# Attention probabilities turned by a DMA transpose of two f16 halves instead of by TensorE, with new periods for all engines

## The chip, the cores and the metric

The kernel runs on one core of one Trainium2 chip. The metric is the device time of one launch in microseconds (us); lower is better.

## What is computed

64 graphs of 128 nodes with 384 features pass through four layers of graph attention with residuals and layer norms. The last two layers (numbers 4 and 5 in the code, parts "c") have 12 heads of 32 features. For each of them the reference does, per graph,

```
score = q @ k.T * scale + bias        # 12 heads, 128 x 128 each
prob  = exp(score - max(score))       # softmax, divided later by its row sum
out_h = prob @ v_h / sum(prob)        # per head
```

All is f32. The kernel gets f32 accuracy from f16 matmuls by splitting each operand in a high half (its f16 rounding) and a low half (the rest, in f16) and adding three products. TensorE (PE) sums over the partitions, so `prob @ v` needs `prob` turned, with the column index on the partitions.

## The kernel before

**Tiling.** One graph is one tile of 128 partitions (nodes) x 384. Its work is cut into streams: "a" and "w" are the first layer pair, "b" and "x" the second, "c" and "y" layers 4 and 5, with small streams for the norms, the masks, the biases and the splits. The 12 heads are handled as four quads j = 0 to 3 of three heads (chunks c = 0 to 2), one PSUM bank (`c_banks[j]`) for a quad.

**Order.** Each engine issues its instructions in the order of a period that is written out as a string in `ORDER`: each letter is the next step of that stream. `FIRST` says in which period and at which place a stream starts, so in one steady period the engines work on steps of about four successive graphs. The function `woven` (L243) issues the periods. An engine runs strictly in this order, so a wait at one step holds all behind it. `WARM_FIRST` and `WARM_LAST` put filler matmuls (L590, L594) into the first and last periods; in the steady part there are none. SyncE (SP), which issues all DMAs, has no period: weights and biases first, then per graph the loads (L268, L273, L278) and the store (L282).

**The steps around the change**, per layer (4 and 5) and graph, with the names of `quad(layer, j)` signals:

- PE L527 makes the scores of the four quads, 24 matmul records for 12 heads.
- VectorE (DVE) L1010 scales them and adds the bias into `score`, L1015 takes the negative row maximum of each head.
- ScalarE (ACT) L739 makes `prob` with Exp, three instructions a quad.
- PE L386 (helper `turned`, called at L534) turns the f32 `prob` of a quad by three transposes into `c_banks[j]`.
- ACT L610 (from L799) copies the bank to f16 as `pt_hi`; DVE L828 (from L1038) writes the rest as `pt_lo`.
- PE L542 to L544 multiply with `v`, nine small matmuls a quad, into bank `c0`; DVE L1042 and L1052 divide by the row sums.

The order within a graph closes a loop: the scores of layer 4 of the next graph wait for `head_out_ready` of layer 5 of this one (L523).

Of the kernel before, what the change touches and what calls it, by code (L numbers as in the profile page):

```python
# [54 lines left out]
def gnn_stack_kernel(nc, x, adj, adj_turned, w_t, biases, norm_rows, beta, out, graphs):  # L55
# [8 lines left out]
    with ctx:  # L64
# [35 lines left out]
        scaled_a, affine_a = (sb(n, [128, D]) for n in ("scaled_a", "affine_a"))  # L100
# [24 lines left out]
        pt_hi = sb("pt_hi", [128, QUADS, CHUNKS, 128], f16)  # L125
        pt_lo = sb("pt_lo", [128, QUADS, CHUNKS, 128], f16)
# [137 lines left out]
        def _(sp):  # L264
# [53 lines left out]
            for m in range(9, N_W):  # L318
                load_weight(m)
# [897 lines left out]
```

## Time and profile before

| | |
|---|---|
| time, median of 3 runs | 2939.22 us (2938.55 to 2939.28) |
| span of the profiled execution | 2938.2 us |
| around the span | 1.0 us, the median less the span |
| PE, DVE, ACT, POOL busy | 2901.9, 2549.3, 2344.3, 393.0 us |
| granted TensorE clock, mean | 0.999 of full |

"Busy" is the share of time in which at least one instruction of the engine runs. Matmuls overlap, so the cost of one is read from the distance between starts in the timeline, not from its duration. Durations of DVE, too, overlap a little with the next one.

### The profile page before, as it was taken

Reading aid. Unit: us, or ns where it says so; the run is one execution under the profiler, and the core shown is the slowest. Engines: PE = TensorE matmul, PEld = TensorE weight load, DVE = VectorE, ACT = ScalarE, POOL = GpSimd, SP = SyncE. Lnnn points to the kernel's source line nnn. Section 1 sums busy time; section 2 is a strip of 40 time slices with the busy share of each in tenths; the row PEclk is TensorE's granted clock in tenths of the full one; section 3 lists DMA queues with packets and bytes.
Section 4 is the critical chain, followed back from the end, with each engine's and each line's share of the span. In section 5 each row is a group of like instructions: output and inputs, shape, how many; then the busy total and the mean of one; then the engine's idle time right before and its main releaser. Section 6 shows DMA issues by size and latency. Waiting matters only on the chain.

```text
span 2938.2 us, 89028 instructions
## 1 busy us (share of the span) xinstructions
PE 2901.9 (99%) x35033; PEld 2323.2 (79%) x35033; DVE 2549.3 (87%) x7450; ACT 2344.3 (80%) x6548; POOL 393.0 (13%) x715
## 2 busy tenths in 40 slices
PE   8999999999999999999999999999999999999998
PEld 6777877877878778787777778778778787787877
DVE  6788888888888898888888888888888888988886
ACT  6788878878878888878888888788788788888775
POOL 1111111111111111111111111111111111111110
PEclk9999999999999999999999999999999999999999
DMA  6000000000000000000000000000000000000000
GB/s 217 11 16 12 14 15 13 14 15 13 13 16 13 13 14 15 13 13 13 16 13 13 15 12 14 15 13 14 15 13 13 16 13 13 13 15 13 13 8 7
DMA packets 48621, 54.21 MB, mean 18 GB/s; under 512 B 5712, under 2 KB 48208, under 8 KB 48208
## 3 DMA queue, kind: packets, MB, share of 16 engines
q1 hardware_dynamic: 48208, 48.52, 5.2%
q8 instruction: 282, 4.62, 0.7%
q14 instruction: 131, 1.07, 0.1%
HBM read 35.92 MB, written 12.58 MB: 17 GB/s over the span
## 4 chain that ended last, share of the span: by engine, by line
PE 94%; DVE 3%; issue 1%; ACT 1%; DMA 1%; SPq 0%; POOL 0%; POOLq 0%; ACTq 0%; DVEq 0%
PE bank_a L340 27%; PE bank_c L340 23%; PE bank_b L340 19%; PE bank_c L386 8%; PE bank_b L372 4%; PE bank_b L379 2%; PE bank_c L527 2%; PE bank_b L386 2%; PE bank_a L386 1%; DVE node_b L968 1%; PE bank_c L543 1%; PE bank_c L542 1%; PE bank_c L544 1%; DVE row_max L860 1%; DMA w_stage<-w_t 1%
## 5 line engine op out<-in xcount | busy, mean ns | idle before, releaser
L739 ACT ACTIVATE prob<-score,neg_head_max 128x128 f32<-128x128 f32 x1536 | 500.0, 390 | 13.7 <-DVE neg_head_max L1015 5.8
L340 PE MATMUL bank_c<-htc_hi,w_hi 128*128 128x128 f16 x2304 | 399.0, 219 | 0.0
L340 PE MATMUL bank_c<-htc_hi,w_lo 128*128 128x128 f16 x2304 | 399.0, 219 | 0.0
L340 PE MATMUL bank_c<-htc_lo,w_hi 128*128 128x128 f16 x2304 | 399.0, 219 | 0.0
L340 PE MATMUL bank_a<-w_hi,hta_hi 128*128 128x384 f16 x1152 | 376.2, 327 | 4.1 <-ACT bank_a L610 4.0
L340 PE MATMUL bank_a<-w_lo,hta_hi 128*128 128x384 f16 x1152 | 375.6, 327 | 0.0
L1010 DVE SCALAR_TENSOR_TENSOR score<-bank_c,bias 128x384 f32<-128x384 f32 x512 | 281.3, 549 | 12.6 <-PE bank_c L527 8.3
L1015 DVE TENSOR_REDUCE neg_head_max<-score 128x3 f32<-128x384 f32 x512 | 281.7, 550 | 9.0
L610 ACT ACTIVATE pt_hi<-bank_c 128x384 f16<-128x384 f32 x512 | 222.3, 483 | 47.8 <-PE bank_c L386 47.8
L828 DVE SCALAR_TENSOR_TENSOR pt_lo<-bank_c,pt_hi 128x384 f16<-128x384 f32 x512 | 258.2, 546 | 2.4 <-ACT pt_hi L610 2.4
L340 PE MATMUL bank_a<-w_hi,hta_lo 128*128 128x384 f16 x1152 | 250.4, 327 | 0.0
L386 PE MATMUL bank_c<-ident,prob 128*128 128x128 f32 x1536 | 240.3, 274 | 3.2 <-ACT prob L739 3.1
L340 PEld LDWEIGHTS bank_c<-htc_lo,w_hi 128*128 128x128 f16 x2304 | 225.3, 98 | 13.1
L340 PEld LDWEIGHTS bank_c<-htc_hi,w_hi 128*128 128x128 f16 x2304 | 225.3, 98 | 12.4
L340 PEld LDWEIGHTS bank_c<-htc_hi,w_lo 128*128 128x128 f16 x2304 | 225.3, 98 | 0.0
L340 PE MATMUL bank_b<-htb_lo,w_hi 128*128 128x128 f16 x1152 | 206.1, 219 | 0.0
L340 PE MATMUL bank_b<-htb_hi,w_hi 128*128 128x128 f16 x1152 | 206.1, 219 | 0.0
L340 PE MATMUL bank_b<-htb_hi,w_lo 128*128 128x128 f16 x1152 | 206.1, 219 | 0.0
L610 ACT ACTIVATE bank_a<-bias_rows 128x384 f32<-128x384 f32 x384 | 189.3, 493 | 21.1 <-DVE hta_lo L831 19.0
L1113 POOL TENSOR_TENSOR rstd_a<-var_eps_a,minus_half 128x1 f32<-128x1 f32 x128 | 71.0, 555 | 984.8 <-DVE var_eps_a L889 984.8
L386 PEld LDWEIGHTS bank_c<-ident,prob 128*128 128x128 f32 x1536 | 176.7, 141 | 31.4 <-issue 11.1
L340 PE MATMUL bank_a<-sides,attn_ta 128*128 128x384 f32 x512 | 195.1, 504 | 0.0
(198 smaller groups left out, 9186.0 us busy)
## 6 DMA issues: line engine op xcount, KB each, us to landing
x_in<-x SPq DMA_DIRECT2D x64, 192.0 KB, 2.4
out<-y_out SPq DMA_DIRECT2D x64, 192.0 KB, 1.8
w_stage<-w_t SPq DMA_DIRECT2D x10, 576.0 KB, 5.9
adj_in<-adj SPq DMA_DIRECT2D x64, 64.0 KB, 2.1
adj_t<-adj_turned SPq DMA_DIRECT2D x64, 64.0 KB, 1.8
score<-w_t SPq DMA_DIRECT2D x5, 576.0 KB, 6.8
prob<-w_t SPq DMA_DIRECT2D x4, 576.0 KB, 7.3
bias_rows<-biases SPq DMA_DIRECT2D x11, 192.0 KB, 7.3
```

The source lines that it names most:

```text
L340: mm = nc.tensor.matmul(out_ap, a, b, start=first and i == 0, stop=last and i == len(pairs_of) - 1, skip_group_check=True)
L372: nc.tensor.matmul(bank[:, cols], w[:, m, c, cols], th[:, c, :], start=(o, c, n) == (0, 0, 0), stop=False, skip_group_check=True)
L379: mm = nc.tensor.matmul(bank[:, cols], w_hi[:, m, c, cols], tl[:, c, :], start=False, stop=(o, c) == (CHUNKS - 1, CHUNKS - 1), skip_group_ ...
L386: mm = nc.tensor.matmul(bank[:, c * 128:(c + 1) * 128], src(c), ident[:, :], start=c == 0, stop=True, is_transpose=True, skip_group_check= ...
L527: mm = nc.tensor.matmul(c_banks[j][:, c * 128:(c + 1) * 128], qk[rows, c, 0, :], qk[rows, c, 1, :], start=True, stop=True)
L542: nc.tensor.matmul(whole, pt_hi[:, j, c, :], v_hi[:, h, :], start=True, stop=False)
L610: return nc.scalar.activation(dst, src, ACT.Copy, scale=scale)
L739: ex = nc.scalar.activation(prob[:, j, c, :], score[:, j, c, :], ACT.Exp, bias=neg_head_max[:, j, c:c + 1])
L828: return V.scalar_tensor_tensor(dst, src, scale, hi, op0=ALU.mult, op1=ALU.subtract)
L1010: V.scalar_tensor_tensor(score[:, j, :, :], chunked(c_banks[j][:, 0:D]), scale, bias[:, :].unsqueeze(1).to_broadcast([128, CHUNKS, 128]), ...
L1015: V.tensor_reduce(neg_head_max[:, j, :], score[:, j, :, :], AX.X, ALU.max, negate=True)\
L1113: P.tensor_tensor(rstd[of][:, :], src, exponent[:, :], ALU.pow).then_inc(root_ready[of][g], 1)
```

## The change

The probabilities are no longer turned by PE. Per quad, DVE copies `prob` from SBUF to the f16 high half in `prob_halves` (new stream "h"), GpSimd (POOL) subtracts and writes the low half beside it (new stream "h"), and SP issues one `dma_start_transpose` of both halves, 128 partitions x 768 f16, from `prob_halves` to `pt_halves` (new stream "t"). PE waits for its landing (`pt_landed[j]`) and multiplies as before. Removed are, per quad, the three PE transposes, the ACT copy `pt_hi` and the DVE instruction `pt_lo`. The banks are now free once the scores are read, so the waits of `start_c` and `biases_c` move from `pt_lo_ready` to `score_ready`. SP gets a period of its own, with the loads, the transposes and the stores in one order. `affine_a` and `affine_b` are dropped; their results are written in place over `scaled_a` and `scaled_b`, whose waits move earlier. The last three weights use only the two stages `w_stage`. All orders, starts and fillers are new: the fillers of the first periods fall from 329 to 242, those of the last rise from 410 to 864.

```diff
+W_PLACE = [m % W_STAGES for m in range(16)] + [m % 2 for m in range(16, N_W)]
+W_BEFORE = [[n for n in range(m) if W_PLACE[n] == W_PLACE[m]] for m in range(N_W)]
...
 ORDER = {
-    "pe": "wwwccxcaxxcaccccxxxcxayybxxawcwybyybyyyyywbcwwwxxxxxcacxxacbccxcctcxybyaybyyyyyacbwww",
-    "act": "wecwcwcppppgnbpbgafiiiembqcxnbaeeciwcccebjjjwccwbpcbcppfpjgbcnnxbaccceaeebc",
-    "dve": "cnacacbczazaappppazapaabapbippppapbbbabcxibaibbcbbabjbcccajccjcccaapqbbaapbppababbcaxbpabc"
-           "bpnbbabcccc",
-    "pool": "acabbqmmabn",
+    "pe": "wwcbyyyyyyyyaxxcxxxxxabxtxyyyybyaycbcayccywwcwwbwwxxxaxxxxacabxxcccawcwyybwwb",
+    "act": "aeenbgwnenmicwqwbjjjccccjbcgbcfcccbxbaecccaeewecbwcwcbcbngafeiiipbx",
+    "dve": "xpbpippaapbbabbbcjbnjjcancccbcchbccchhaahabcababbaxbqabbabbpcbapacccachcbchcchazhbabaazaaa"
+           "zaipbbapbib",
+    "pool": "haammqcbnbhhhahbhhh",
+    "sp": "ultttttttts",
 FIRST = {
...
+    "pe": {"a": (0, 6), "b": (2, 0), "c": (3, 6), "t": (3, 0), "w": (0, 8), "x": (2, 0), "y": (3, 8)},
+    "act": {"a": (0, 3), "b": (2, 1), "c": (3, 9), "e": (0, 7), "f": (2, 0), "g": (3, 1), "i": (1, 1), "j": (3, 0), "m": (4, 0), "n": (0, 0), "p": (3, 0), "q": (3, 0), "w": (1, 0), "x": (2, 0)},
+    "dve": {"a": (0, 22), "b": (2, 6), "c": (3, 10), "h": (3, 4), "i": (1, 1), "j": (3, 0), "n": (0, 0), "p": (3, 7), "q": (3, 0), "x": (2, 1), "z": (3, 0)},
+    "pool": {"a": (1, 2), "b": (2, 2), "c": (4, 0), "h": (3, 5), "m": (2, 0), "n": (0, 0), "q": (3, 0)},
+    "sp": {"l": (0, 0), "s": (4, 0), "t": (3, 4), "u": (2, 0)},
...
-        pt_hi = sb("pt_hi", [128, QUADS, CHUNKS, 128], f16)
-        pt_lo = sb("pt_lo", [128, QUADS, CHUNKS, 128], f16)
+        prob_halves = sb("prob_halves", [128, QUADS, 2, CHUNKS, 128], f16)
+        pt_halves = sb("pt_halves", [128, QUADS, 2, CHUNKS, 128], f16)
...
-        pt_done, pt_hi_ready, pt_lo_ready = Signal("pt_done", 8), Signal("pt_hi_ready", 8), Signal("pt_lo_ready", 8)
+        prob_hi_ready, prob_lo_ready = Signal("prob_hi_ready", 8), Signal("prob_lo_ready", 8)
+        pt_landed = [Signal(f"pt_landed{j}", 2, 16) for j in range(QUADS)]
...
-                if m >= W_STAGES:
-                    sp.wait_ge(w_lo_split, m - W_STAGES + 1)
-                sp.dma_start(w_stage[m % W_STAGES], w_t[m, :, :].rearrange("(c p) n -> p c n", p=128))\
-                    .then_inc(w_loaded[m % W_STAGES], 16)
+                if W_BEFORE[m]:
+                    sp.wait_ge(w_lo_split, W_BEFORE[m][-1] + 1)
+                sp.dma_start(w_stage[W_PLACE[m]], w_t[m, :, :].rearrange("(c p) n -> p c n", p=128))\
+                    .then_inc(w_loaded[W_PLACE[m]], 16)
...
+            def turn_probabilities(g):
+                for l in range(2):
+                    for j in range(QUADS):
+                        sp.wait_ge(*prob_lo_ready.at(g, quad(4 + l, j)))
+                        sp.dma_start_transpose(pt_halves[:, j, :, :, :].rearrange("p h c n -> p (h c) n"),
+                                               prob_halves[:, j, :, :, :].rearrange("p h c n -> p (h c n)"))\
+                            .then_inc(pt_landed[j][g], 16)
+                        yield
...
+            woven("sp", later_weights(), l=stream(loads), u=stream(loads_turned), t=stream(turn_probabilities), s=stream(stores))
...
-                    pe.wait_ge(*pt_lo_ready.at(g - 1, quad(5, 3)))
+                    pe.wait_ge(*score_ready.at(g - 1, quad(5, 3)))
...
-                                                  qk[rows, c, 1, :], start=True, stop=True)
+                                                  qk[rows, c, 1, :], start=c == 0, stop=True, skip_group_check=True)
                             if c == CHUNKS - 1:
                                 mm.then_inc(score_done[g], 1)
                     yield
                     for j in range(QUADS):
-                        pe.wait_ge(*prob_ready.at(g, quad(layer, j)))
-                        turned(c_banks[j], lambda c: prob[:, j, c, :]).then_inc(pt_done[g], 1)
-                        yield
-                    for j in range(QUADS):
-                        pe.wait_ge(*pt_hi_ready.at(g, quad(layer, j)))
-                        pe.wait_ge(*pt_lo_ready.at(g, quad(layer, j)))
+                        pe.wait_ge(*pt_landed[j].at(g, k))
                         for c in range(CHUNKS):
                             h = QUADS * c + j
                             whole = c0[:, h * (HEAD + 1):(h + 1) * (HEAD + 1)]
-                            nc.tensor.matmul(whole, pt_hi[:, j, c, :], v_hi[:, h, :], start=True, stop=False)
-                            nc.tensor.matmul(whole, pt_lo[:, j, c, :], v_hi[:, h, :], start=False, stop=False)
-                            mm = nc.tensor.matmul(c0[:, h * (HEAD + 1):h * (HEAD + 1) + HEAD], pt_hi[:, j, c, :],
+                            nc.tensor.matmul(whole, pt_halves[:, j, 0, c, :], v_hi[:, h, :], start=True, stop=False)
+                            nc.tensor.matmul(whole, pt_halves[:, j, 1, c, :], v_hi[:, h, :], start=False, stop=False)
+                            mm = nc.tensor.matmul(c0[:, h * (HEAD + 1):h * (HEAD + 1) + HEAD], pt_halves[:, j, 0, c, :],
...
             def turned_c(g):
-                for l in range(2):
-                    for j in range(QUADS):
-                        act.wait_ge(*pt_done.at(g, quad(4 + l, j)))
-                        copy(pt_hi[:, j, :, :], chunked(c_banks[j][:, 0:D]), scale=1.0).then_inc(pt_hi_ready[g], 1)
-                        yield
-                    if l == 0:
-                        act.wait_ge(*ot_done.at(g))
-                        copy(ot_hi[:, :, :], chunked(c1[:, 0:D]), scale=1.0).then_inc(ot_hi_ready[g], 1)
-                        yield
+                act.wait_ge(*ot_done.at(g))
+                copy(ot_hi[:, :, :], chunked(c1[:, 0:D]), scale=1.0).then_inc(ot_hi_ready[g], 1)
+                yield
 
...
+                    if l == 0 and g:
+                        dve.wait_ge(*x1_ready.at(g - 1))
...
-                    dst = (node_a, affine_a)[l]
+                    dst = (node_a, scaled_a)[l]
                     done = (node_a_ready, affine_a_ready)[l]
-                    if l == 1 and g:
-                        dve.wait_ge(*x1_ready.at(g - 1))
...
+                    if g == 0 and l == 0:
+                        dve.wait_ge(w_lo_split, 16)
+                    if l:
+                        dve.wait_ge(*zero_test_ready.at(g))
...
+            def probabilities_high(g):
+                for l in range(2):
+                    for j in range(QUADS):
+                        dve.wait_ge(*prob_ready.at(g, quad(4 + l, j)))
+                        V.tensor_copy(prob_halves[:, j, 0, :, :], prob[:, j, :, :]).then_inc(prob_hi_ready[g], 1)
+                        yield
...
-                    for j in range(QUADS):
-                        dve.wait_ge(*pt_hi_ready.at(g, quad(layer, j)))
-                        lo_part(pt_lo[:, j, :, :], chunked(c_banks[j][:, 0:D]), pt_hi[:, j, :, :], 1.0)\
-                            .then_inc(pt_lo_ready[g], 1)
-                        yield
...
+            def halves_c(g):
+                for l in range(2):
+                    for j in range(QUADS):
+                        pool.wait_ge(*prob_hi_ready.at(g, quad(4 + l, j)))
+                        P.tensor_tensor(prob_halves[:, j, 1, :, :], prob[:, j, :, :], prob_halves[:, j, 0, :, :], ALU.subtract)\
+                            .then_inc(prob_lo_ready[g], 1)
+                        yield
```

## Rows read from the trace of the kernel before

**Rows 1.** Stretch 1000 to 1500 us: length, busy us of PE, PEld, DVE, ACT, POOL; clock.

```profile
1000.00:1500.00 500.00, 498.06 (x6007) 398.95 (x6006) 442.92 (x1306) 406.78 (x1144) 67.64 (x122) 1.00 0.04 14
```

**Rows 2.** Tile view of `y_out`, 500 to 2500 us: min/median/max ns, first and last start.

```profile
L1077 DVE TENSOR_TENSOR y_out<-head_out,x x45: 522/525/559, 504.9 to 2463.9; 128x384 f32<-128x384 f32 x45
```

**Rows 3.** The only wait of PE for a probability: total us, times, longest.

```profile
PE bank_c L386 <- ACT prob L739: 3.1, 6, 0.7
```

**Rows 4.** Groups by line: busy us, mean ns of one, idle before.

```profile
L739 ACT ACTIVATE prob<-score,neg_head_max 128x128 f32<-128x128 f32 x1536 | 500.0, 390 | 13.7 <-DVE neg_head_max L1015 5.8
L610 ACT ACTIVATE pt_hi<-bank_c 128x384 f16<-128x384 f32 x512 | 222.3, 483 | 47.8 <-PE bank_c L386 47.8
L828 DVE SCALAR_TENSOR_TENSOR pt_lo<-bank_c,pt_hi 128x384 f16<-128x384 f32 x512 | 258.2, 546 | 2.4 <-ACT pt_hi L610 2.4
```

**Rows 5.** Timeline of PE: start us, duration us, matmuls merged.

```profile
1511.85 0.95 PE L527 MATMUL bank_c<-qk 32*128 32x128 f32 x24
1512.73 0.34 PE L340 MATMUL bank_a<-w_hi,hta_hi 128*128 128x384 f16 x1
1512.90 0.33 PE L340 MATMUL bank_a<-w_lo,hta_hi 128*128 128x384 f16 x1
...
1516.02 0.67 PE L379 MATMUL bank_b<-htb_lo,w_hi 128*128 128x128 f16 x9
1516.52 0.22 PE L340 MATMUL bank_b<-htb_hi,w_hi 128*128 128x128 f16 x1
...
1517.03 0.50 PE L386 MATMUL bank_c<-ident,prob 128*128 128x128 f32 x3
1517.36 0.27 PE L421 MATMUL bank_a<-ident,attn_a 128*128 128x128 f32 x1
...
1518.80 1.51 PE L340 MATMUL bank_a<-sides,attn_ta 128*128 128x384 f32 x4
1520.15 0.49 PE L386 MATMUL bank_c<-ident,prob 128*128 128x128 f32 x3
1520.48 0.27 PE L340 MATMUL bank_b<-m_hi,htb_hi 128*128 128x256 f16 x1
1520.59 0.27 PE L340 MATMUL bank_b<-m_lo,htb_hi 128*128 128x256 f16 x1
```

**Rows 6.** Timeline of DVE, 1537.9 to 1541 us, full without a wait.

```profile
1537.90 0.94 DVE L1024 TENSOR_REDUCE head_min<-score 128x6 f32<-128x768 f32 x1
1538.76 0.41 DVE L878 TENSOR_TENSOR attn_ta<-bank_a,upper_lower 128x256 f32<-128x256 f32 x1
1539.09 0.15 DVE L882 SCALAR_TENSOR_TENSOR den_eps<-den_a 128x1 f32<-128x1 f32 x1
1539.16 1.95 DVE L828 SCALAR_TENSOR_TENSOR pt_lo<-bank_c,pt_hi 128x384 f16<-128x384 f32 x4
1541.03 0.55 DVE L834 BATCH_NORM_STATS2 stats_a<-bank_a 128x6 f32<-128x384 f32 x1
```

**Rows 7.** Groups by line of POOL, of 128 columns.

```profile
L1136 POOL TENSOR_TENSOR tri_mask<-adj_t,upper_lower 128x128 f32<-128x128 f32 x64 | 29.2, 456 | 0.0
L1159 POOL MEMSET upper_lower<- 128x256 f32 x1 | 0.3, 315 | 0.0
L1160 POOL MEMSET upper_incl<- 128x128 f32 x1 | 0.2, 204 | 0.0
```

**Rows 8.** DMA issues of the whole execution: KB each, median us to landing.

```profile
out<-y_out SPq DMA_DIRECT2D x64, 192.0 KB, 1.8
```

**Rows 9.** DMA view, 95 to 100 us, one `adj_t`: packets, MB, share of 16 engines.

```profile
q1 hardware_dynamic: 144, 0.07, 4.6%
```

**Rows 10.** DMA view, 1529 to 1535 us, one store of `y_out`.

```profile
q1 hardware_dynamic: 144, 0.20, 8.8%
```

**Rows 11.** Timeline of POOL, then of DVE, near 1529 us.

```profile
1528.93 0.77 POOL L1113 TENSOR_TENSOR rstd_b<-mean_var_b,plus_half 128x1 f32<-128x1 f32 x1 [5.12 <-DVE mean_var_b L837]
1529.67 0.54 POOL L1113 TENSOR_TENSOR rstd_in<-var_eps_in,minus_half 128x1 f32<-128x1 f32 x1
...
1528.77 0.53 DVE L1077 TENSOR_TENSOR y_out<-head_out,x 128x384 f32<-128x384 f32 x1
```

More of the change, by code:

```diff
@@ L99, in gnn_stack_kernel @@
         sides = sb("sides", [128, 2, D])
-        scaled_a, affine_a = (sb(n, [128, D]) for n in ("scaled_a", "affine_a"))
+        scaled_a = sb("scaled_a", [128, D])
         row_max, neg_max, z_sum, edge_sum, d_sum, den_a, den_eps = (
@@ L298, in load_biases, with loads, loads_turned, stores @@
                     sp.dma_start(bias_rows[:, n, :], biases[m:m + 1, :].to_broadcast([128, D])).then_inc(bias_loaded[i], 16)
+            def turn_probabilities(g):
[6 more added lines that the diff above has]
+                        yield
+            def loads(g):
+                if g >= 2:
+                    load(g)
+                yield
+            def loads_turned(g):
+                if g:
+                    load_turned(g)
+                yield
+            def stores(g):
+                store(g)
+                yield
             load(0)
@@ L317, in _, with later_weights, stream @@
             load_biases(2, 6, len(BIASED))
-            for m in range(9, N_W):
-                load_weight(m)
-            for i in range(2):
-                m = W_INDEX[5] + 1 + i
-                for c in range(CHUNKS):
-                    sp.dma_start(qk_bias[:, i, c:c + 1], biases[m:m + 1, c * 128:(c + 1) * 128].rearrange("a p -> p a"))\
-                        .then_inc(qk_bias_loaded, 16)
-            for g in range(2, graphs):
-                load(g)
-                load_turned(g - 1)
-                if g >= 4:
-                    store(g - 4)
-            load_turned(graphs - 1)
-            for g in range(max(graphs - 4, 0), graphs):
-                store(g)
+            def later_weights():
+                for m in range(9, N_W):
+                    load_weight(m)
+                    yield
+                for i in range(2):
+                    m = W_INDEX[5] + 1 + i
+                    for c in range(CHUNKS):
+                        sp.dma_start(qk_bias[:, i, c:c + 1], biases[m:m + 1, c * 128:(c + 1) * 128].rearrange("a p -> p a"))\
+                            .then_inc(qk_bias_loaded, 16)
+                yield
+            def stream(steps):
+                for g in range(graphs):
+                    yield from steps(g)
+            woven("sp", later_weights(), l=stream(loads), u=stream(loads_turned), t=stream(turn_probabilities), s=stream(stores))
             for g in range(max(graphs - 2, 0), graphs):
@@ L777, in biases_c @@
                 if g:
-                    act.wait_ge(*pt_lo_ready.at(g - 1, quad(5, 1)))
+                    act.wait_ge(*score_ready.at(g - 1, quad(5, 1)))
                 bias(c1, 8, g, bias_c_set)
                 yield
-                act.wait_ge(*pt_lo_ready.at(g, quad(4, 2)))
+                act.wait_ge(*score_ready.at(g, quad(4, 2)))
                 bias(c2, 9, g, bias_c_set)
@@ L795, in turned_c @@
             def turned_c(g):
[L796 to L804 removed]
+                act.wait_ge(*ot_done.at(g))
+                copy(ot_hi[:, :, :], chunked(c1[:, 0:D]), scale=1.0).then_inc(ot_hi_ready[g], 1)
+                yield
             def split_high(m):
[L807 to L808 removed]
+                act.wait_ge(w_loaded[W_PLACE[m]], 16 * (len(W_BEFORE[m]) + 1))
+                nc.scalar.activation(w_hi[:, m, :, :], w_stage[W_PLACE[m]], ACT.Copy, scale=W_SCALE).then_inc(w_hi_split, 1)
             def later_weights():
@@ L910, in end_a @@
                     dve.wait_ge(*x2_ready.at(g - 2, 1))
-                V.scalar_tensor_tensor(x1[g % 2][:, :], affine_a[:, :], 0.0, x_in[g % 2][:, :], op0=ALU.max, op1=ALU.add)\
+                V.scalar_tensor_tensor(x1[g % 2][:, :], scaled_a[:, :], 0.0, x_in[g % 2][:, :], op0=ALU.max, op1=ALU.add)\
                     .then_inc(x1_ready[g], 1)
@@ L952, in chain_b @@
                     dve.wait_ge(*mean_ready["b"].at(g, k))
+                    if l == 0 and g:
+                        dve.wait_ge(*x2_ready.at(g - 1, 1))
                     V.scalar_tensor_tensor(scaled_b[:, :], b0[:, 0:D], mean_var["b"][:, 0:1], norms[:, 2 * layer, :],
@@ L963, in chain_b @@
                     dve.wait_ge(*scaled_b_ready.at(g, k))
-                    dst = (node_b[1], affine_b)[l]
+                    dst = (node_b[1], scaled_b)[l]
                     done = (node_b_ready, affine_b_ready)[l]
-                    if l == 1 and g:
-                        dve.wait_ge(*x2_ready.at(g - 1, 1))
                     V.scalar_tensor_tensor(dst[:, :], scaled_b[:, :], inv_sd[:, :], norms[:, 2 * layer + 1, :],
@@ L981, in end_b @@
                     dve.wait_ge(*y_ready.at(g - 2))
-                V.scalar_tensor_tensor(x2[g % 2][:, :], affine_b[:, :], 0.0, x1[g % 2][:, :], op0=ALU.max, op1=ALU.add)\
+                V.scalar_tensor_tensor(x2[g % 2][:, :], scaled_b[:, :], 0.0, x1[g % 2][:, :], op0=ALU.max, op1=ALU.add)\
                     .then_inc(x2_ready[g], 1)
```

24 lines of the change are left out of this document (14 added, 10 removed), and 20 rows, old and new, of tables (FIRST, WARM_FIRST, WARM_LAST).

## Prediction

> **What bounds the kernel now.** I read the page's busy shares first and then one steady stretch: of 500 us PE is busy 498.06, DVE 442.92, ACT 406.78, POOL 67.64, at full clock [rows 1]. The list of waits says the same from the other side: PE waited for a probability 3.1 us in the whole execution [rows 3]. So PE is the bound, and everything that it issues costs time. The length of a period comes from `y_out`: 45 stores from 504.9 to 2463.9, so 1959.0 / 44 = 44.52 us a graph [rows 2]. 64 of them are 2849.3 us; of the span of 2938.2, 88.9 are left for the edges, where the pipeline fills and drains. The third view is the timeline of PE, where distances of starts give the issue cost: three transposes of `prob` hold PE from 1517.03 to 1517.36, 0.33 us; nine f16 matmuls of 128 columns 0.50; one of 384 columns 0.165; one of 256 0.11; a context product 1.35; the scores 0.88 [rows 5].
>
> **Taken away.** PE: 8 quads x 0.33 = 2.64 us a graph [rows 5], all on the bound. ACT: 222.3 / 64 = 3.5 us a graph; DVE: 258.2 / 64 = 4.0 [rows 4]. Neither shortens the period by itself, as both lie beside PE's work, but they take two engines out of the way from `prob` to the product.
>
> **Added on DVE.** Eight copies f32 to f16 of 384 columns. The trace has no such copy; its cost lies between a one-column instruction, 0.07, and the start distance of 384 columns, 0.47 (four from 1539.16 to 1541.03) [rows 6]. I take 0.47, the nearest row: 3.8 us a graph. DVE's 442.92 / 500 x 44.52 = 39.4 us becomes 39.4 - 4.0 + 3.8 = 39.2, below PE's new 41.9.
>
> **Added on POOL.** Eight subtractions of 384 columns. A two-input instruction of 128 columns took 0.456 us; memsets of 128 and 256 columns 0.204 and 0.315, so about 0.09 is fixed [rows 7]. Bounds: three times 0.456 = 1.37, and 0.456 + 256 columns at the memset's 0.87 ns = 0.68. Scaling only the part that is not fixed gives 0.09 + 3 x 0.366 = 1.18, taken. POOL goes from 6.0 to 15.4 us of a period, so it is not the bound. But its inverse roots stand behind the subtractions in its order, and DVE waits for these.
>
> **Added on SP and the DMA queue.** Eight transposes a graph of 192 KB each, where the trace has none. A store of 192 KB lands after 1.8 us [rows 8]. What the queue spends comes from packets: 144 for `adj_t` took 4.6% of 16 engines x 5 us, 25.6 ns each at 455 bytes on average; 144 for `y_out` 8.8% of 16 x 6 us, 58.7 ns at 1365 bytes [rows 9, 10]. That is some 9 ns a packet and 0.036 ns a byte. The store thus holds the engines 9 x 58.7 ns = 0.53 us, and 1.27 us of its landing are fixed. For a transpose I write T for the time that it holds the engines; alone it lands after T + 1.27. If it moves in pieces of 256 bytes (128 columns of f16), each engine has 48 pieces of 18 ns: T = 0.9, landing 2.1 us. In pieces of 32 bytes it has 384 of 10 ns: T = 3.9. In single elements 6144 of 9 ns: T = 56. The low end is a store, 0.53. I take 0.9: rows of 256 contiguous bytes are what the destination pattern names. All ends are kept.
>
> The rows thus make it 0.9 for all six 128 x 128 blocks of a transpose. The Trainium skill, "VectorE: DVE Perf Modes", The three transpose paths, gives 1309 ns for one 128 x 128 bf16 block turned by DMA and recommends TensorE where PSUM will do. If that scales with the blocks, T is an estimated 7.9 and the kernel takes about twice its time (the last rival says how); if it is mostly a fixed part, it agrees with the rows. No run of before shows a transpose by DMA.
>
> **How late may it land?** This decides, because PE waits in order. In the new PE order I add issue costs from the end of a layer's scores to the product of the last quad. Layer 5: `x` 0.33, 0.5, three of 0.5; `a` 1.35; `b` 0.98; `x` 0.65; `t` 0.33; `x` 0.81; `y` 0.65, 0.81, three of 0.5; `b` 0.11; `a` 0.33; `y` 0.5; this reaches quad 0 after 10.35, and with 0.23 for each product, `b` 0.49, `a` 0.5 and `y` 0.5 quad 3 after 12.5. Layer 4 likewise: quad 0 after 7.7, quads 1 to 3 at 10.7 to 11.2.
>
> In DVE's order, from the first score of layer 4 to the end of the fourth copy, there are 13 instructions of 384 columns (four scores, four maxima, `htb_lo`, four copies), one `head_min` of 0.86, one `attn_ta` of 0.33 and one small: 6.1 + 1.26 + 0.1 for its end = 7.4 us [rows 6]. ACT's three Exps, 500.0 / 1536 = 0.33 us apiece [rows 4], run beside it. POOL adds 1.18: 8.6. So the fourth transpose has 11.2 - 8.6 = 2.6 us to land, and needs 2.1. In layer 5 (15 instructions of 384 columns) it is ready after 8.4 and has 4.1 us. The first quads are ready after 3.7 (five instructions of 384 columns, then POOL) and 4.6 us (seven). In these four gaps only the fourth quad of layer 4 is tight. The loads stand ahead of the transposes in SP's order; x and adjacency are needed a part of a period later, so that a wait of theirs is covered; the store stands last, and the load of the next graph behind it has most of a period.
>
> **The other edits** cost nothing: the dropped `affine` tiles make waits on `x1_ready` and `x2_ready` one step earlier, for results of the period before; two weight stages for the last three weights and the new SP order concern the first four periods; the score matmuls' flags add no instruction.
>
> **The sum.** 44.52 - 2.64 = 41.88 us a period, x 64 = 2680.3. Edges: 88.9, and the fillers go from 739 to 1106, 367 more x 0.0556 = 20.4, as they stand where PE would be idle: 109.3. Together 2789.6. Then the tight quad: between 0 (it lands in 2.1) and 0.8 us a period (subtraction 1.37, packets a little longer, a POOL instruction held up). I take 0.4: 25.6 us. 2815 of span, 2816 with the 1.0 around it.
>
> **Rivals.**
>
> *DVE and POOL hold each other up.* A one-column root on POOL took 0.77 us beside DVE's `y_out`, which reads two SBUF tiles, and 0.54 right after it [rows 11]. POOL now reads SBUF 9.4 us a graph more. If each of the eight subtractions delays one DVE instruction by half its length, DVE gets 39.2 + 8 x 0.59 = 43.9 us and becomes the bound: 64 x 43.9 + 109 = 2919, faster by little. Against: most DVE instructions read one operand from PSUM. The Trainium skill, "SBUF — State Buffer", SBUF: two separate sides, calls the shared port pair an exclusive lock for the whole instruction; the row's 0.2 us agrees in kind.
>
> *The transposes queue up.* This ends on the other side. If T is above about 1.5, the four of a layer follow each other, and the last lands 3.7 + 4T + 1.27 after the scores of layer 4, 4.6 + 4T + 1.27 after those of layer 5. PE stands 4T - 6.2 and 4T - 6.7 us. Together this eats the 2.64 from T = 1.94 on. T = 2.1 gives 41.88 + 3.9 = 45.8 us, 3040; T = 2.3 gives 47.4, 3143. For it: 48 pieces an engine with an unknown fixed part each. Against: 256-byte pieces at the rows' prices give less than half.
>
> *Pieces of 32 bytes.* T = 3.9, stands 9.4 and 8.9, 60.2 us a period: 3962.
>
> *Block by block.* A transpose holds six blocks of 128 x 128. If each pays the fixed 1.27 us before the next starts, T = 6 x (1.27 + 0.15) = 8.5, stands 27.8 and 27.3, 97 us a period: 6317. The page on the three transpose paths (the Trainium skill, "VectorE: DVE Perf Modes") would by the same sum give an estimated 6010. No row here speaks for such a T; single elements, T = 56, would be ten times slower still.
>
> **How the numbers follow.** Forecast 0.52, own range 2785 to 2870. DVE and POOL 0.09 (2870 to 2930). Queueing with T of 1.8 to 2.3: 0.19 (2885 to 3150; 0.02 still faster, 0.02 the same). 32 bytes 0.12, block by block or worse 0.06. Below 2775: 0.02. The range 2775 to 3150 leaves out 0.20. 0.2% (5.9 us) is about what a measurement of this kernel can tell from no change. Faster 0.52 + 0.09 + 0.02 + 0.02 = 0.65, same 0.02, slower 0.15 + 0.12 + 0.06 = 0.33.
>
> **What the profile after would show.** No L386 with `prob`; `y_out` spaced 42.3 us; PE waits only at the product of layer 4, on the DMA; DMA landing of 2 to 2.7 us; POOL subtractions near 1.2 us; DVE copies at or below 0.55; DVE busy near 93% of the steady part. Wrong would make it: landings above 3 us, growing from quad to quad (queueing); long `prob_lo` waits on SP with short landings (POOL or DVE late); roots on POOL behind subtractions with DVE waiting; or edges well over 110 us.

## The result: 1.5% slower

The changed kernel takes 2984.64 us (median of 4 runs, 2983.7 to 2986.2), the kernel before 2939.25 (4 runs, 2938.55 to 2939.98): a ratio of 1.0154 [1.0139, 1.0168]. The forecast was 2816 and faster. The time is inside the range given, but the direction is wrong, and what made it so is none of the slower cases that the prediction worked out.

The profiled execution took 2984.4 us, with a span of 2982.6. First the page of the kernel after, its busy times, and the stretch that answers to [rows 1], with the same columns:

```profile
PE 2845.0 (95%) x33864; PEld 2130.4 (71%) x33864; DVE 2593.1 (87%) x7450; ACT 2096.4 (70%) x6036; POOL 846.5 (28%) x1227
...
1000.00:1500.00 500.00, 478.29 (x5650) 355.72 (x5649) 446.05 (x1291) 356.71 (x1037) 146.85 (x212) 1.00 0.24 49
```

PE, which had 498.06 of 500 us busy, now has 478.29: in the steady part it waits for 4% of the time. DVE is at 446 of 500, POOL at 147. The clock is full in both, so it has no part in this. The chain that ended last, by engine, of the kernel after:

```profile
DVE 58%; PE 25%; ACT 6%; issue 6%; POOL 3%; DMA 2%; SPq 0%; DVEq 0%; ACTq 0%; POOLq 0%
```

Before, the same line gave PE 94% and DVE 3%. The bound has moved from PE to DVE, although DVE still has time left over. The tile view of `y_out`, as in [rows 2]:

```profile
L1105 DVE TENSOR_TENSOR y_out<-head_out,x x45: 550/553/558, 515.2 to 2495.6; 128x384 f32<-128x384 f32 x45
```

(2495.6 - 515.2) / 44 = 45.01 us a graph, against 44.52 before. 64 of these are 2880.6, and 102 us are left for the edges. So all of the loss is in the period.

What the change added, from the groups by line and the DMA issues of the page, and from the tile view of `pt_halves` (issue on SP as min/median/max ns, then its landing):

```profile
L1190 POOL TENSOR_TENSOR prob_halves<-prob,prob_halves 128x384 f16<-128x384 f32 x512 | 469.1, 922 | 959.1 <-DVE prob_halves L1049 959.1
L1049 DVE CAST prob_halves<-prob 128x384 f16<-128x384 f32 x512 | 194.8, 391 | 1.6 <-ACT prob L767 1.5
...
q1 hardware_dynamic: 457808, 149.25, 24.1%
```
```profile
L313 SPq DMA_TRANSPOSE pt_halves<-prob_halves x512: 1209/1217/2582, 114.1 to 2974.0; - x171
...
DMA to landing us min/median/max: 2.7/2.8/4.9
```

Each is near what was forecast, and the landings don't grow from quad to quad. What PE waits for, in the steady 500 us of the kernel after (total us, times, longest):

```profile
PE bank_c L373 <- DVE htc_lo L853: 8.6, 12, 0.7
PE bank_b L502 <- DVE attn_b L967: 7.0, 12, 0.6
PE bank_b L373 <- DVE m_lo L850: 2.1, 11, 0.2
PE bank_c L570 <- DMA pt_halves<-prob_halves: 0.5, 1, 0.5
```

Before, this list was empty for the same stretch. The DMA is one wait of 0.5 us. The two large waits are for DVE, in steps of which the change edits nothing. DVE's groups of that stretch say where DVE is late:

```profile
L904 DVE SCALAR_TENSOR_TENSOR den_eps<-den_a 128x1 f32<-128x1 f32 x22 | 16.5, 751 | 0.0
L960 DVE CUSTOM_DVE_ANT_0 delta_b<-expo_b,adj_in 128x128 f32<-128x128 f32 x23 | 15.1, 657 | 0.0
```

The same two in the kernel before:

```profile
L882 DVE SCALAR_TENSOR_TENSOR den_eps<-den_a 128x1 f32<-128x1 f32 x23 | 3.4, 149 | 0.0
L938 DVE CUSTOM_DVE_ANT_0 delta_b<-expo_b,adj_in 128x128 f32<-128x128 f32 x22 | 6.3, 286 | 4.1 <-ACT expo_b L694 4.1
```

A multiplication of one column per partition now takes 0.75 us. The mean of `delta_b` hides two kinds, as its tile view after shows (min/median/max ns):

```profile
L960 DVE CUSTOM_DVE_ANT_0 delta_b<-expo_b,adj_in x23: 281/997/1005, 1002.3 to 1497.5; 128x128 f32<-128x128 f32 x23
```

Of the two in a period one takes its 0.28 us as before, with POOL idle, and the other 1.0 us. The timelines of DVE, of POOL, and of PE's two waits in one period show why (start us, duration us, and in brackets the idle time and its releaser):

```profile
1538.34 0.62 DVE L1049 CAST prob_halves<-prob 128x384 f16<-128x384 f32 x2
1538.87 0.88 DVE L904 SCALAR_TENSOR_TENSOR den_eps<-den_a 128x1 f32<-128x1 f32 x1
1539.67 0.55 DVE L856 BATCH_NORM_STATS2 stats_a<-bank_a 128x6 f32<-128x384 f32 x1
1540.14 0.67 DVE L1049 CAST prob_halves<-prob 128x384 f16<-128x384 f32 x1
...
1541.14 0.54 DVE L853 SCALAR_TENSOR_TENSOR htc_lo<-bank_c,htc_hi 128x384 f16<-128x384 f32 x1
...
1542.40 1.00 DVE L960 CUSTOM_DVE_ANT_0 delta_b<-expo_b,adj_in 128x128 f32<-128x128 f32 x1
...
1543.64 0.29 DVE L967 TENSOR_SCALAR attn_b<-delta_b,r_den_b 128x128 f32<-128x128 f32 x1
```
```profile
1538.77 1.83 POOL L1190 TENSOR_TENSOR prob_halves<-prob,prob_halves 128x384 f16<-128x384 f32 x2 [1.33 <-DVE prob_halves L1049]
1541.83 0.55 POOL L1141 TENSOR_TENSOR rstd_a<-var_eps_a,minus_half 128x1 f32<-128x1 f32 x1 [1.23 <-DVE var_eps_a L911]
1542.34 0.91 POOL L1190 TENSOR_TENSOR prob_halves<-prob,prob_halves 128x384 f16<-128x384 f32 x1
```
```profile
1541.74 0.66 PE L373 MATMUL bank_c<-w_hi,htc_lo 128*128 128x384 f16 x3 [0.72 <-DVE htc_lo L853]
1543.99 0.33 PE L502 MATMUL bank_b<-ident,attn_b 128*128 128x128 f32 x1 [0.58 <-DVE attn_b L967]
```

POOL starts two subtractions at 1538.77, the second about half-way through the 1.83 us, at 1539.69. DVE's `den_eps`, started at 1538.87, ends at 1539.75, with the first of them. `delta_b` starts at 1542.40, 0.06 us behind a subtraction that ends at 1543.25, and ends at 1543.40. It is the long one of its period; the short one, at 1521.02, has no POOL instruction beside it. The cast at 1540.14, beside the second one, takes 0.67 instead of about 0.35. What stands behind in DVE's order is late by it: `htc_lo`, for which PE stands 0.72 us, and `attn_b`, for which it stands 0.58. In [rows 6] `den_eps` took 0.15, and POOL had nothing beside it.

The Trainium skill, "SBUF — State Buffer", SBUF: two separate sides, names the kinds: a DVE instruction with two SBUF inputs and a GpSimd instruction that reads SBUF exclude each other for a whole instruction. These timelines agree; the experiments test whether it is this or POOL's being late.

### The profile page after: what moved, and what is told of

It is laid out like the page before. It is cut to its first block, busy times and chain, and to the rows that moved or that the text cites. A ratio compares the mean times of both kernels' runs of the same rounds, so it can differ in the third digit from the quotient of the medians.

```text
span 2982.6 us, 86753 instructions
## 1 busy us (share of the span) xinstructions
PE 2845.0 (95%) x33864; PEld 2130.4 (71%) x33864; DVE 2593.1 (87%) x7450; ACT 2096.4 (70%) x6036; POOL 846.5 (28%) x1227
## 3 DMA queue, kind: packets, MB, share of 16 engines
q1 hardware_dynamic: 457808, 149.25, 24.1%
## 4 chain that ended last, share of the span: by engine, by line
DVE 58%; PE 25%; ACT 6%; issue 6%; POOL 3%; DMA 2%; SPq 0%; DVEq 0%; ACTq 0%; POOLq 0%
PE bank_c L373 13%; DVE neg_head_max L1041 9%; DVE score L1036 8%; DVE prob_halves L1049 4%; DVE m_lo L850 4%; DVE head_min L1057 3%; DVE den_eps L904 3%; PE bank_c L560 2%; DVE delta_b L960 2%; DVE stats_a L856 2%; PE bank_b L373 2%; PE bank_a L373 2%; PE bank_b L405 2%; ACT node_b L643 1%; DMA pt_halves<-prob_halves 1%
## 5 line engine op out<-in xcount | busy, mean ns | idle before, releaser
L1190 POOL TENSOR_TENSOR prob_halves<-prob,prob_halves 128x384 f16<-128x384 f32 x512 | 469.1, 922 | 959.1 <-DVE prob_halves L1049 959.1
L373 PE MATMUL bank_c<-htc_hi,w_lo 128*128 128x128 f16 x2304 | 405.5, 219 | 0.0
L373 PE MATMUL bank_c<-htc_lo,w_hi 128*128 128x128 f16 x2304 | 405.5, 219 | 0.0
L638 ACT ACTIVATE m_hi<-bank_b 128x384 f16<-128x384 f32 x256 | 124.3, 486 | 117.3 <-PE bank_b L412 102.3
L373 PE MATMUL bank_b<-htb_hi,w_hi 128*128 128x128 f16 x1152 | 199.6, 219 | 0.0
L373 PE MATMUL bank_b<-htb_lo,w_hi 128*128 128x128 f16 x1152 | 199.6, 219 | 0.0
L373 PE MATMUL bank_b<-htb_hi,w_lo 128*128 128x128 f16 x1152 | 199.6, 219 | 0.0
L1049 DVE CAST prob_halves<-prob 128x384 f16<-128x384 f32 x512 | 194.8, 391 | 1.6 <-ACT prob L767 1.5
L373 PE MATMUL bank_c<-w_hi,htc_hi 128*128 128x384 f16 x576 | 188.8, 329 | 0.3 <-issue 0.2
L373 PE MATMUL bank_c<-w_lo,htc_hi 128*128 128x384 f16 x576 | 187.4, 326 | 0.0
```

What stands on the lines that cost most here:

```text
L373: mm = nc.tensor.matmul(out_ap, a, b, start=first and i == 0, stop=last and i == len(pairs_of) - 1, skip_group_check=True)
L638: return nc.scalar.activation(dst, src, ACT.Copy, scale=scale)
L1049: V.tensor_copy(prob_halves[:, j, 0, :, :], prob[:, j, :, :]).then_inc(prob_hi_ready[g], 1)
L1190: P.tensor_tensor(prob_halves[:, j, 1, :, :], prob[:, j, :, :], prob_halves[:, j, 0, :, :], ALU.subtract)\
```

## The experiments

The accounts were: DVE and POOL hold each other up; the transposes are the cost; POOL's mere length delays the landing; DVE, or a stretch of ACT, has too much work in this order. Periods are worked out as above, from the spacing of `y_out`.

**e1: POOL writes and reads nothing.** The low half is left out: two memsets of it stand for the subtraction, for about the same time.

```diff
-P.tensor_tensor(prob_halves[:, j, 1, :, :], prob[:, j, :, :], prob_halves[:, j, 0, :, :], ALU.subtract)\
-    .then_inc(prob_lo_ready[g], 1)
+P.memset(prob_halves[:, j, 1, :, :], 0.0).then_inc(spare_set, 1)
+pool.wait_ge(spare_set, g * 8 + l * 4 + j + 1)
+P.memset(prob_halves[:, j, 1, :, :], 0.0).then_inc(prob_lo_ready[g], 1)
```

> The changed kernel with each POOL subtraction replaced by two memsets of the low half (zeros; the low half of the probabilities is left out), so that POOL is about as long at work (some 0.9 us) but reads nothing from SBUF. Theory A (a POOL instruction that reads SBUF and a DVE instruction with two SBUF inputs shut each other out): the stretched DVE rows go back to their length before (den_eps 0.15 instead of 0.75 us, delta_b 0.29 instead of 0.66, the cast 0.35 instead of 0.39), which frees about 2.3 us of DVE a period; the period falls from 45.0 to 43 or less and the kernel to 2845 to 2870 us. Theory B (the new order's waits between engines set the period, not the shut-out): the rows shrink, but the period stays above 44.5 us, 2950 or more.

Measured: 2884.96 us, 0.9814 [0.9797, 0.983] of the kernel before; period 43.36. The groups of DVE, then of POOL, 1000 to 1500 us:

```profile
L961 DVE CUSTOM_DVE_ANT_0 delta_b<-expo_b,adj_in 128x128 f32<-128x128 f32 x23 | 6.4, 278 | 0.0
L905 DVE SCALAR_TENSOR_TENSOR den_eps<-den_a 128x1 f32<-128x1 f32 x23 | 3.5, 152 | 0.0
```
```profile
L1191 POOL MEMSET prob_halves<- 128x384 f16 x92 | 42.7, 465 | 172.7 <-DVE prob_halves L1050 172.7
L1193 POOL MEMSET prob_halves<- 128x384 f16 x92 | 38.5, 418 | 5.3
```

POOL is busy as long as before, 465 + 418 = 883 ns against 922, behind the same casts, and `den_eps` and `delta_b` are back at 152 and 278 ns. The period falls by 1.65 us, which still leaves it 1.5 above PE's own 41.88, and the time above the 2845 to 2870 us expected. For these two instructions it is therefore what POOL reads, not how long it works, and this by itself turns the sign: without it the change is 1.9% faster. Not everything goes back, though. One cast of the eight in a period still takes 0.53 us instead of 0.35 beside a memset, and one of the two `attn_b` 0.39 instead of 0.29. Both instructions go from SBUF to SBUF, and POOL only writes here.

**e2: POOL is short.** The same with one memset of two elements a quad (119 ns), the rest of the low half set to zero once at the start.

```diff
+P.memset(prob_halves[:, j, 1, 0, 0:2], 0.0).then_inc(prob_lo_ready[g], 1)
```

> The changed kernel with each POOL subtraction replaced by a memset of two elements (the low half is left zero). It takes away the shut-out and also POOL's 0.9 us ahead of each transpose. Theory A: within 10 us of the run with long memsets, since POOL's length is not on the chain. Theory C (the way from score to product is what is too long): clearly faster than the run with long memsets, by up to 2 x 0.8 us a period, 100 us.

Measured: 2864.75 us, 0.9742 [0.9728, 0.9757]; period 43.03. The expectation of theory A, within 10 us of e1, missed: it is 20 us faster. The 43.36 - 43.03 = 0.33 us a period are the price of POOL's length, together with the small stretches that its writing leaves in e1 (the longest cast is 0.36 us here, the longest `attn_b` 0.29). Where most of it goes can be seen: from 500 to 2500 us, 46 periods, PE's weight loads wait 9.8 us for landings in e1 and not once in e2.

```profile
PEld bank_c L571 <- DMA pt_halves<-prob_halves: 9.8, 19, 0.8
```

That is 0.21 us a period.

**e3: `den_eps` in another form.** The whole computation. The second factor becomes a pointer scalar, so that the instruction has one tensor input.

```diff
-V.scalar_tensor_tensor(den_eps[:, :], den_a[:, :], 1e-12, den_a[:, :], op0=ALU.mult, op1=ALU.mult)\
+V.tensor_scalar(den_eps[:, :], den_a[:, :], 1e-12, den_a[:, :], ALU.mult, ALU.mult)\
```

> The changed kernel, complete, with one DVE instruction written in another form: den_eps as a tensor_scalar with den_a as a per-partition scalar instead of a scalar_tensor_tensor with den_a as two SBUF inputs. Same place, same result. Theory A: its mean falls from 0.75 to about 0.15 to 0.2 us, two a period, 1.1 us less on DVE; the kernel gets 40 to 70 us faster, 2915 to 2945. Theory B: the row falls but the time stays within 10 us of 2984.

Measured: 2919.98 us, 0.9931 [0.9916, 0.9946]; period 43.97. DVE's groups, 1000 to 1500 us:

```profile
L960 DVE CUSTOM_DVE_ANT_0 delta_b<-expo_b,adj_in 128x128 f32<-128x128 f32 x23 | 14.4, 627 | 0.0
L904 DVE TENSOR_SCALAR den_eps<-den_a 128x1 f32<-128x1 f32 x22 | 4.5, 206 | 0.0
```

`den_eps` gives back 751 - 206 = 0.545 us twice a period, 1.09, and the period falls by 1.04. `delta_b` is still held. One line, on one column, is worth 2.2% of the kernel (2984.64 to 2919.98).

**e4: half of the transpose.** The low half is not turned and stays zero.

```diff
-sp.dma_start_transpose(pt_halves[:, j, :, :, :].rearrange("p h c n -> p (h c) n"),
-                       prob_halves[:, j, :, :, :].rearrange("p h c n -> p (h c n)"))\
+sp.dma_start_transpose(pt_halves[:, j, 0, :, :],
+                       prob_halves[:, j, 0, :, :].rearrange("p c n -> p (c n)"))\
```

> The changed kernel with only the high half turned (three blocks a transpose instead of six); the low half in pt_halves stays zero, so its product adds nothing. POOL and DVE work as before. Theory A: the landing is not on the chain but in a few waits; the issue on SP and the landing get shorter, and the time stays within 15 us of 2984. Theory D (the transposes are too slow for their gaps): 50 us faster or more.

Measured: 2981.38 us, 1.0138 [1.0123, 1.0153]; period 45.01 as in the kernel after. Its queue and its landing:

```profile
q1 hardware_dynamic: 261200, 98.92, 13.6%
...
DMA to landing us min/median/max: 2.3/2.3/4.4
```

Half the data, and a landing 0.5 us earlier, change next to nothing (3 us of the time, nothing of the period). The transposes are not what makes this kernel slow.

**e5: `expo_b` in PSUM too.** The whole computation. With e3's edit, ACT writes `expo_b` into a free part of a PSUM bank, so that `delta_b` reads one operand from SBUF instead of two.

```diff
-        u_sum, expo_b, delta_b, attn_b = (
-            sb(n, [128, 128]) for n in ("u_sum", "expo_b", "delta_b", "attn_b"))
+        u_sum, delta_b, attn_b = (sb(n, [128, 128]) for n in ("u_sum", "delta_b", "attn_b"))
...
+        expo_b = b1[:, 256:384]
```

> Complete. The den_scalar form, and expo_b moved from SBUF to free columns of bank b1 in PSUM, so that delta_b has one SBUF input. Theory A: delta_b falls from 0.63 to about 0.3 us (0.7 us a period on the chain), den_eps stays at 0.2; the kernel gets 30 to 45 us faster than den_scalar: 2875 to 2890, near the 2885 of the long memsets. Theory B': another DVE instruction with two SBUF inputs takes the collision over and the time stays above 2905.

Measured: 2888.36 us, 0.9821 [0.9804, 0.9839]; period 43.40. It beats both kernels. Its stretch, and the group of `delta_b` in it:

```profile
1000.00:1500.00 500.00, 492.14 (x5897) 370.22 (x5896) 439.75 (x1327) 370.37 (x1076) 152.37 (x218) 1.00 0.26 50
```
```profile
L960 DVE CUSTOM_DVE_ANT_0 delta_b<-bank_b,adj_in 128x128 f32<-128x128 f32 x23 | 6.4, 278 | 0.0
```

With POOL's subtractions as they are, 936 ns each, two operands taken out of the way bring what e1 brought by taking POOL's reads away: 43.40 against 43.36. These two instructions thus carry nearly all of the hold-up that costs time. The price of the second can be followed: the long `delta_b` gives back 1.00 - 0.28 = 0.72 us once a period. But POOL still subtracts there, and now `attn_b` behind it takes 0.42 us instead of 0.29. The 0.59 left is what the period falls by, 0.57. One tensor operand in SBUF and a pointer scalar are thus held too, but much less.

**e6, e7, e8: the work on other engines.** In e6 (on top of e5) ACT makes the high half right behind its Exps and DVE doesn't; in e7 DVE makes both halves and POOL none; in e8 ACT makes the high half and DVE the low one. All three are the whole computation.

```diff
 # e6 and e8, ACT; DVE's tensor_copy is left out
+act.wait_ge(*prob_ready.at(g, quad(layer, j)))
+copy(prob_halves[:, j, 0, :, :], prob[:, j, :, :], scale=1.0).then_inc(prob_hi_ready[g], 1)
 # e7 and e8, DVE; POOL's tensor_tensor is left out
+dve.wait_ge(*prob_hi_ready.at(g, quad(4 + l, j)))
+V.tensor_tensor(prob_halves[:, j, 1, :, :], prob[:, j, :, :], prob_halves[:, j, 0, :, :], ALU.subtract)\
+    .then_inc(prob_lo_ready[g], 1)
```

> Complete. As expo_psum, and the high half is copied by ACT right after the Exps of a quad (with a wait for their end) instead of by DVE. DVE loses 8 x 0.27 to 0.35 us a period, ACT gains 8 x 0.5 and a wait each. If DVE is what the chain still runs over: 20 to 60 us faster than expo_psum. If the order of steps sets the rest: within 15 us of it, or slower because ACT comes later to its next step.

> Complete. The changed kernel with the subtraction on DVE right behind the cast, none on POOL: no shut-out, but 8 x (0.47 and a wait of 0.1) us more on DVE. DVE at 40.15 - 2.3 + 4.6 = 42.5 us busy and with the same waits a period of 45.5 to 47.5: 3015 to 3140 us. If the shut-out cost more than what the list of stretched rows shows, it comes out under 2985.

> Complete. The changed kernel with the high half on ACT and the low half on DVE, none on POOL. DVE at 40.15 - 2.3 - 2.8 + 3.8 = 38.9 us, ACT 4 us more, no shut-out: 2870 to 2930 us. If DVE's waits and not its work count: like the changed kernel without shut-out, 2885.

Measured: e6 3089.1 us, 1.0507 [1.0488, 1.0525], period 46.63; e7 3141.13, 1.0683 [1.0666, 1.07], 47.44; e8 3124.05, 1.0624 [1.0607, 1.0641], 47.18. Groups of DVE in e7, then in e6, 1000 to 1500 us, and a piece of DVE's timeline in e7:

```profile
L1051 DVE TENSOR_TENSOR prob_halves<-prob,prob_halves 128x384 f16<-128x384 f32 x87 | 48.6, 558 | 3.0
```
```profile
L852 DVE SCALAR_TENSOR_TENSOR m_lo<-bank_b,m_hi 128x384 f16<-128x384 f32 x44 | 24.4, 555 | 20.2 <-ACT m_hi L638 19.1
L855 DVE SCALAR_TENSOR_TENSOR htc_lo<-bank_c,htc_hi 128x384 f16<-128x384 f32 x22 | 12.2, 554 | 20.4 <-ACT htc_hi L738 20.4
```
```profile
1522.03 0.35 DVE L1049 CAST prob_halves<-prob 128x384 f16<-128x384 f32 x1
1522.41 0.56 DVE L1051 TENSOR_TENSOR prob_halves<-prob,prob_halves 128x384 f16<-128x384 f32 x1
1522.89 0.35 DVE L1049 CAST prob_halves<-prob 128x384 f16<-128x384 f32 x1
```

In e7 a cast and its subtraction hold DVE from 1522.03 to 1522.89, 0.86 us, where a cast alone holds it 0.27 in the kernel after. That adds 8 x 0.59 = 4.7 us to what e2 has, and the period is 4.41 longer than e2's, so its time, 3141, is just beyond the expected range. DVE work put behind the casts thus lies on the path almost one for one, at a period of which DVE fills 89% (446 of 500 us after, 447 in e7). The share alone doesn't say so: DVE had 443 of 500 in the kernel before, where PE waited for nothing. e6 missed: DVE has less to do (392 of 500 us busy), but waits 20.4 us for `htc_hi` and 19.1 for `m_hi`, which stand on ACT behind eight copies of 523 ns that the order has no place for. e8 missed likewise; there DVE waits 22.4 us for ACT's copies themselves. An order written for one division of work doesn't show what another division is worth; these two say nothing against ACT for a kernel whose order is made anew.

**e9, e10, e11: a stretch of ACT.** What is left after e5 is 43.40 - 41.88 = 1.52 us. DVE waits for ACT's sum in the norm of x, and I took that ACT stretch for the cause. On top of e5, e9 puts a spare ACT copy of 256 columns into it, e10 the same copy elsewhere, and e11 makes it lighter (the sums of the input norm over 16 columns only, the others left out).

```diff
 # e9 and e10, at two places
+copy(spare[:, 0:256], upper_lower[:, :, :].rearrange("p a n -> p (a n)")).then_inc(spare_set, 1)
 # e11
+w = 16 if of == "in" else D
-nc.scalar.activation(spent[of][:, :], src[:, :], ACT.Copy, accum_out=total[of][:, :])
+nc.scalar.activation(spent[of][:, 0:w], src[:, 0:w], ACT.Copy, accum_out=total[of][:, :])
```

> Complete, expo_psum plus one spare ACT copy of 256 columns a period (about 0.35 us), put before the moments of x2 (L648 spent_bc), in the stretch where ACT works without a gap between DVE's x1 and the scores of PE. Theory E (what is left above PE's own 41.9 us a period is a loop DVE, ACT, PE, DVE through this stretch): the period grows by about as much, 0.35 us, and the kernel by 20 to 25 us to about 2911. Rival F (PE alone is the bound again): within 6 us of 2888.

> Complete, expo_psum plus the same spare copy, put before the bias of bank a that waits 2 us for DVE's hta_lo. Theories E and F: ACT is idle there, within 6 us of 2888. If any ACT work counts: 2911 as in the other place.

> expo_psum with the two passes of ACT over x_in (mean and squares of the first norm) on 16 columns instead of 384; this leaves out most of that norm's statistics. About 0.8 us less in the full ACT stretch. Theory E: the period falls by 0.5 to 0.8 us until another loop or PE bounds it: 2835 to 2860. Rival F: within 6 us of 2888.

Measured: 2886.65 us, 0.982 [0.9806, 0.9835]; 2890.18, 0.9831 [0.9814, 0.9847]; 2886.1, 0.9816 [0.9801, 0.9831]. All three are e5 again. More or less work in that stretch does nothing: the theory (E) falls. That PE alone is the bound (F) doesn't follow from it: the period is still 1.5 us above PE's own work.

**e12: `den_eps` in its old form, at another place.** The whole computation. It keeps its two SBUF inputs but stands one step earlier, right behind `den_a`, not behind the casts.

```diff
+                    dve.wait_ge(*den_a_ready.at(g, k))
+                    V.scalar_tensor_tensor(den_eps[:, :], den_a[:, :], 1e-12, den_a[:, :], op0=ALU.mult, op1=ALU.mult)\
+                        .then_inc(den_eps_ready[g], 1)
                     yield
...
-                    dve.wait_ge(*den_a_ready.at(g, k))
-                    V.scalar_tensor_tensor(den_eps[:, :], den_a[:, :], 1e-12, den_a[:, :], op0=ALU.mult, op1=ALU.mult)\
-                        .then_inc(den_eps_ready[g], 1)
```

> Complete. The changed kernel with den_eps in its old form, but issued one step of its stream earlier (right behind den_a), where no subtraction runs on POOL. Theory A: den_eps is back at 0.15 us with its two SBUF inputs, and the time equals the tensor_scalar form within 15 us: 2905 to 2935. If the form of the instruction mattered and not the collision: it stays slow at the new place and the time at 2984.

Measured: 2918.0 us, 0.9927 [0.9912, 0.9941]; period 43.93. DVE's group, 1000 to 1500 us:

```profile
L899 DVE SCALAR_TENSOR_TENSOR den_eps<-den_a 128x1 f32<-128x1 f32 x23 | 3.7, 159 | 0.8
```

The same instruction, unchanged, takes 159 ns where POOL has nothing to subtract (one starts at 1517.34, POOL's next subtraction at 1518.31), and the kernel is e3's. It is the meeting of the two, not the form of the instruction.

## Why the prediction was wrong

**The account.** Per period: 44.52 before; less 2.64 for PE's transposes, 41.88; plus 1.04 for `den_eps` (after to e3), 0.57 for `delta_b` (e3 to e5) and 0.04 that lies between e5 and e1, 1.65 together; plus 0.33 for POOL's length and what its writing stretches (e1 to e2); plus 1.15 that is left in e2. The sum is 45.01. Against the forecast of 42.28 (41.88 and 0.4) it is 2.73 more, 174.7 us over 64 periods, less 7 us of edges: the 167 us between a span of 2815 and one of 2982.6.

**The step that failed** is the rival "DVE and POOL hold each other up", with its chance of 0.09 and its price. It named the mechanism, with the row that shows it [rows 11], but dismissed it on an average ("most DVE instructions read one operand from PSUM") and priced it as busy time: eight half subtractions on top of 39.2 us, giving 43.9 as a new bound. Neither holds. Which instructions are hit is not a matter of chance, as the order is the same in every period. Both `den_eps` stand behind a cast, one directly and one with `m_lo` between, and POOL subtracts beside them. The `delta_b` that is held is the seventh instruction behind its cast; there POOL's subtraction comes late, because the root `rstd_a` ahead of it in POOL's order waits for DVE's `var_eps_a`. So a look at what follows each `h` in DVE's order would have found `den_eps`, and the two orders side by side were needed for `delta_b`. And the price is the delay of what stands behind them on the way to PE, not DVE's sum: 0.6 us on a one-column instruction cost 0.5 us of the period each time (e3), and DVE's whole busy sum with the hold-up in it, 40.15 us, stayed far below the 43.9.

**The premise beneath it** failed as well: "DVE 39.2, below PE's new 41.9", so PE sets the period. DVE has 40.15 us busy a graph (446.05 / 500 x 45.01). The size is near by luck: the hold-up is in it, and without it DVE has 38.1 (439.55 / 500 x 43.36 in e1), as the casts were priced too high. But in the new order DVE had no slack at the steps that PE waits for, and e7 shows work put behind the casts on the path almost one for one. The order before left PE no wait for DVE in the stretch looked at. I carried that over to a new order at a period 2.6 us shorter. With the hold-up alone added to the forecast it would be 42.28 + 1.65 = 43.93 a period and 2921 us, still faster; it took both to turn the sign.

**What is left, 1.15 us,** is located in part and not explained. In e5 PE's weight loads show waits at many places (whole execution: total us, times, longest; "issue" means that the profile shows nothing that was waited for):

```profile
PEld bank_b L373 <- issue: 70.4, 127, 1.1
PEld bank_c L373 <- ACT htc_hi L738: 29.7, 124, 0.3
PEld bank_c L419 <- DVE head_out L1080: 22.9, 64, 0.4
PEld bank_c L570 <- DMA pt_halves<-prob_halves: 20.7, 34, 1.5
...
PEld bank_b L419 <- ACT node_b L643: 18.5, 62, 0.3
...
PEld bank_c L373 <- DVE htc_lo L853: 14.4, 62, 0.4
PEld bank_c L419 <- ACT node_c L643: 14.0, 64, 0.6
```

A wait of the weight loads isn't all lost, as PE may still be multiplying. Before, these lists had `head_out` with 0.3 us, `node_c` with 1.7 and `htc_hi` with 10.3. In the rows with ACT or DVE, PE has turned or multiplied something and needs ACT's or DVE's result of it sooner than it has other work to fill the time. The first row has two places a period. One can be read in PE's timeline of e5:

```profile
1009.47 1.51 PE L373 MATMUL bank_a<-sides,attn_ta 128*128 128x384 f32 x4
1011.17 0.27 PE L373 MATMUL bank_b<-m_hi,htb_hi 128*128 128x256 f16 x1 [0.20 <-DVE m_lo L850]
```

The next instruction comes 1.70 us behind the start of the context product, where it came after 1.35 in [rows 5]: 0.35 us a period, and the wait that the profile names there is for DVE's `m_lo`. This place is under a third of the 1.15 us, the others weren't priced, and e9 to e11 exclude the ACT stretch that I suspected. Whether another order would recover it was not tried.

**Point by point.** Right: PE's 2.64 (its other matmuls kept their start distances); in the kernel after, no product waiting for the DMA to speak of (0.5 us in 500); pieces near 256 bytes and T near 0.9, measured (24.1 - 5.2)% x 2982.6 / 512 = 1.10 us of the 16 engines for each transpose, 5.2% being the queue's share before; hence no queueing from quad to quad, no 32-byte pieces, no block by block; edges 102 against 109. Right by luck: the 0.4 taken for the tight fourth quad, beside the 0.33 of e1 to e2. The waits for a landing that e1 and e5 show come in some graphs only, nearly all at landings of 4.2 to 4.7 us instead of 2.8 and mostly at the first quad of layer 4, which the prediction held to be safe; why some transposes land that late isn't shown. Mis-sized: the cast, 0.39 in busy time (0.27 between starts) against 0.47; the subtraction, 0.92 against 1.18; the landing, 2.8 against 2.1, of which the issue alone takes 1.2 us, where that of a store took 0.34. Wrong: `y_out` at 42.3 (45.01), DVE near 93% (89%), and PE waiting only at the product of layer 4. The sign named for "roots on POOL behind subtractions with DVE waiting" came true only in small: DVE waits 7.3 us in 500 for one root. The queue rival that carried most of the slower chance had no part.

## What to carry to other kernels

When work is moved to POOL, list which DVE instructions with two SBUF inputs stand in the order where POOL will be reading SBUF, however small they are, and move them, give them a pointer scalar, or keep one operand in PSUM. Lay POOL's order beside DVE's for this, as POOL's instruction may come late: e5 removes these meetings with two small edits and turns 1.5% slower into 1.8% faster (0.9821 [0.9804, 0.9839]). Cost such a meeting as a delay of everything behind it in that engine's order, not as an addition to its busy sum. And don't take an engine near 90% of the new period for free because another is above it: in one order it cost PE nothing, in the next its work was on the path. A gain on the first engine is worth only what the other engines' order lets through, here 2.64 - 1.15 - 0.33 = 1.16 us with no hold-up at all.

## What the runs showed of the hardware

- DVE's one-column `den_eps` took 149 ns alone and 751 ns on average beside a POOL subtraction; with a pointer scalar it took 206, and beside POOL memsets 152. `delta_b`, of 128 columns, took 281 ns alone and 1.00 us beside a subtraction, and with one of its two inputs in PSUM 275 beside one.
- `attn_b`, 128 columns from SBUF to SBUF with a pointer scalar, took 0.29 us alone, 0.39 beside a POOL memset (e1) and 0.42 beside a subtraction (e5).
- A transpose by DMA of six 128 x 128 blocks of f16 landed in 2.8 us (median; 41 of the 357 issued from 500 to 2500 us took over 4), of three in 2.3 (e4), and held the engines for 1.10 and (13.6 - 5.2)% x 2980.4 / 512 = 0.49 us. The Trainium skill, "VectorE: DVE Perf Modes", The three transpose paths, gives 1309 ns for one block; three more blocks cost 0.5 us of landing here, so the figure doesn't scale with the blocks.
- SP was held 1.2 us to issue one transpose, almost the same for half the data (1180 against 1217 ns), where a store of 192 KB took it 0.34 us in the kernel before and 0.58 in this one.
- A copy from f32 to f16 of 384 columns took ACT 523 ns in e6, DVE 350 ns in e7, where POOL reads nothing beside it.
